# Local attention of a two-layer decoder: in five of its first seven rounds the tensor engine's projections and second arguments stand ahead of the gathers

## The reference, cut to what matters

```python
g = x @ Wg.T + bg                      # 16 heads of 32
v = x @ Wv.T + bv
dot = einsum('bhid,bhjd->bhij', g, g)
corr = dot / (|g_i| * |g_j| + 1e-8) * m        # m: j <= i and j >= i - 128
corr = (corr + 1) / 2
denom = mean_j(corr) + 0.5
fitness = 1 / (denom * sum_i(1 / denom))
attn = softmax(corr * fitness * m + (1 - m) * NEG)
out = (attn @ v) @ Wo.T + bo
```

## Time and profile before

| | |
|---|---|
| Median of 3 runs | 2631.18 us (2628.03 to 2631.48) |
| The profiled execution, whole | 2634.46 us |
| Its span in the trace | 2632.7 us |
| PE busy | 2500.4 us, 95% of the span |
| DVE busy | 2004.3 us, 76% |
| POOL, ACT busy | 864.7 us, 669.0 us |
| Local attention's tiles on PE (arguments) | from 963.4 to 1481.3 us |
| The seven filling rounds | from 963.4 to about 1019.9 us |

### The profile page before, as it was taken

One profiled execution on the slowest core, in us unless ns is written; L12 is line 12 of the kernel. 1 busy time (PEld: TensorE's weight loads), 2 busy tenths in 40 slices (PEclk: granted clock), 3 DMA queues, 4 the chain that ended last, 5 costly groups with the idle time before them and its releaser, 6 DMA issues. The chain is left out here.

```text
span 2632.7 us, 37028 instructions
## 1 busy us (share of the span) xinstructions
PE 2500.4 (95%) x12485; PEld 1550.3 (59%) x12485; DVE 2004.3 (76%) x3404; ACT 669.0 (25%) x961; POOL 864.7 (33%) x900
## 2 busy tenths in 40 slices
PE   8999998999998888999998879999999999999998
PEld 3444544666655434454544447777777777777775
DVE  4899504888877446777778859888888888888886
ACT  1000222222223125666668611000000000000000
POOL 2332103555554336676777611111111111111000
PEclk9999999999999999999999989999999999999999
DMA  6455132222210375555544431222222222222111
GB/s 177 150 167 160 54 108 56 57 59 55 56 41 1 79 152 126 132 130 130 140 111 138 137 101 45 53 54 54 54 55 52 52 52 52 54 54 54 46 39 38
DMA packets 506921, 219.02 MB, mean 83 GB/s; under 512 B 298191, under 2 KB 473679, under 8 KB 505710
## 3 DMA queue, kind: packets, MB, share of 16 engines
q1 hardware_dynamic: 458198, 185.11, 27.6%
q10 hardware_dynamic: 48536, 31.54, 4.7%
HBM read 104.93 MB, written 66.85 MB: 65 GB/s over the span
## 5 line engine op out<-in xcount | busy, mean ns | idle before, releaser
L2216 PE MATMUL bank<-tiles,tl_XQT 128*128 128x512 f32 (+1 forms) x768 | 323.4, 564 | 1.2 <-issue 1.2
L2221 PE MATMUL bank<-tiles,tl_XQT 128*128 128x512 f32 (+1 forms) x768 | 318.0, 557 | 0.0
L2233 PE MATMUL bank<-tiles,tl_HT 128*128 128x512 f32 x682 | 300.8, 596 | 6.0 <-DMA tl_HT<-tl_tmp 6.0
L2216 PEld LDWEIGHTS bank<-tiles,tl_XQT 128*128 128x128 f32 x768 | 235.6, 309 | 79.3 <-issue 15.3
L2221 PEld LDWEIGHTS bank<-tiles,tl_XQT 128*128 128x128 f32 x768 | 236.9, 308 | 65.4
L2233 PEld LDWEIGHTS bank<-tiles,tl_HT 128*128 128x128 f32 x682 | 219.3, 324 | 73.2 <-issue 7.9
L2295 ACT ACTIVATE tl_HQ<-bank 128x512 f32<-128x512 f32 (+1 forms) x96 | 54.0, 562 | 802.1 <-PE bank L2216 756.2
L1493 POOL TENSOR_SCALAR_AFFINE_SELECT tiles<-tiles 128x512 f32<-128x512 f32 x256 | 182.0, 714 | 171.5 <-ACT tiles L1725 154.5
L2163 POOL TENSOR_TENSOR tl_rs<-tl_ve,mhalf 128x1 f32<-128x1 f32 x29 | 16.0, 550 | 526.2 <-DVE tl_ve L2374 526.2
L1498 POOL TENSOR_SCALAR_AFFINE_SELECT tiles<-tiles 128x512 f32<-128x512 f32 x224 | 154.0, 687 | 0.0
L1824 DVE SCALAR_TENSOR_TENSOR tiles<-tiles,bank 128x1024 f32<-128x1024 f32 (+1 forms) x128 | 141.7, 1148 | 15.2 <-PE bank L1600 14.3
(11 more groups left out here) (303 smaller groups left out, 4630.7 us busy)
## 6 DMA issues: line engine op xcount, KB each, us to landing
tl_HT<-tl_tmp SPq DMA_DIRECT2D x248, 44.0 KB, 1.9
tl_HT<-tl_tmp ACTq DMA_DIRECT2D x248, 44.0 KB, 2.0
fp_weights<-space_quant ACTq DMA_DIRECT2D x132, 64.0 KB, 2.0
X<-in_x SPq DMA_DIRECT2D x8, 1024.0 KB, 11.1
v<-tiles SPq DMA_DIRECT2D x32, 256.0 KB, 2.4
unit_g<-tiles SPq DMA_DIRECT2D x32, 256.0 KB, 2.5
unit_gT<-tiles SPq DMA_DIRECT2D x128, 64.0 KB, 2.4
la_GN<-unit_g SPq DMA_DIRECT2D x128, 64.0 KB, 2.1
```

The costliest lines, as they stand in the source:

```text
L2216: mm = e.matmul(bank[(2 * q) % 3][:, 0:w], chunk(XQT[n % 2], c), WgT[q][:, :, c, :], start=(c == 0), stop=(c == C - 1))
L2221: mm = e.matmul(bank[(2 * q + 1) % 3][:, 0:w], chunk(XQT[n % 2], c), WuT[q][:, :, c, :], start=(c == 0), stop=(c == C - 1))
L2233: mm = e.matmul(of_chunks(bank[DOWN][:, :]), chunk(HT, q), WdT[:, q], start=(q == 0), stop=(q == IC - 1))
```

## The change

A round is now a *ramp* round if it prepares tiles, attends to none and isn't late. That holds for rounds 0, 2, 4, 8 and 12. In these, on the tensor engine alone, the projection comes directly behind the first argument, then the second argument, and only then the two gathers. Rounds 6 and 10, and all from round 14 on, keep their order. No instruction is added or removed, and no other engine's list changes.

```diff
                     for n, h in chains:
                         if n is not None:
                             sums(n, h, p)
+
+                    ramp = there(p) and not there(x) and not late
+                    if ramp:
+                        projections(*projected(p), s)
+                        arguments(p + 1)
                     if there(p - 2):
                         gather(p - 2)
                         gather(p - 1)
...
                     if there(x):
                         attend(x)
-                    if there(p):
-                        arguments(p + 1)
-                    projections(*projected(p), s)
+                    if not ramp:
+                        if there(p):
+                            arguments(p + 1)
+                        projections(*projected(p), s)
                     if s in product_at:
                         local_out(product_at[s])
```

## The result

| | before | changed |
|---|---|---|
| Median of 7 runs each | 2631.48 us (2628.03 to 2632.45) | 2640.80 us (2636.34 to 2642.15) |
| Ratio, with its 95% interval | 1 | 1.0031 (1.0022 to 1.0041) |
| Span of the profiled execution | 2632.7 us | 2640.3 us |

The ratio makes +8.2 us (+5.8 to +10.8). I had forecast 2630.7 and a range up to 2635.0. The direction came out as my rival C, to which I had given 7%. The two traces come from long executions: the one of the changed kernel took 2642.15 us, the highest of its seven, and the one of before 2634.46 us, above all seven of before. So traces are compared here by stretches, and whole times by the ratio.

The account below looks back on a forecast made before the run. The tensor engine, busy 95% of 2632.7 us, was taken as the bound. Start-time terms of -7.0, +2.0, +0.8, +4.2 and -0.5 gave -0.5 us, applied to the median 2631.2 for 2630.7 us, range 2627.0 to 2635.0.

Parts of the forecast that it names:

- rival C: Round 12: the clock falls behind two new holes, for scores and dots 2, +5.6 us to 2636.8; chance 7%.
- the one on the clock: Round 2: full clock since the hole ahead shrinks; nothing in the sum, +2.1 us kept for the range.
- rival B: Round 2 or one later hole: the clock is low there, giving 2632.8 to 2634.7 us; chance 23%.
- The fixed point: Round 2: the load of GN1 lets gather 1 start at 976.02, before and after the change.
- Round 0, gain 0: Argument 2 still comes at about 970.5: 1.12 us idle goes, but it must wait for tanh 1.
- Rounds 4 to 10: Lead falls from 7.0 to 5.0 us in round 6 and 4.2 at dots 0; nothing covers z's latency.
- Round 12: Gathers queue behind the g product waiting for scores; gather 11 ends 9.15 us behind the dots, lead 0.
- +4.2 and -0.5: Round 12: the lead of 4.2 us is given back, then dots 2 and 3 end about 0.5 us earlier.
- The sum of the order, -0.5 us: Chain over rounds 0 to 12: terms of -7.0, +2.0, +0.8, +4.2 and -0.5 us; chance 56%.
- the lead of 7.0: Round 2: argument 4 starts at 976.5 against 983.50, 6.0 us of it from the v product.

Follow-up runs that it names:

- The kernel with all holes filled: Changed kernel plus idle products, whose result nobody reads, in all its holes on the tensor engine: ratio to before 1.0009 (1.0000 to 1.0018).
- the kernel with the bias first in all rounds: Changed kernel with unit, bias and turned unit ahead of z on the vector engine in rounds 0, 4, 8 and 12: ratio to before 0.9991.
- the filled kernel before: Kernel before, nothing moved, idle products added ahead of gathers 1 and 9 and between arguments 0 and 1, 10 and 11: ratio to before 1.0000.
- the two filled changed kernels: Changed kernel with idle products in most holes, ratio to before 1.0017, and with more between neighbouring arguments, in all holes, 1.0009.
- The experiment with the bias ahead of z: Changed kernel with unit, bias and turned unit ahead of z on the vector engine in round 12 alone: ratio to before 1.0003 (0.9994 to 1.0013).
- round 2 alone: Kernel before with the new order in round 2 only: ratio to before 1.0007; profiled a second time in one execution, 2629.35 us.

## Why the prediction was wrong, point by point

**The step that failed is the one on the clock**, "I take the better value, since the hole of 4.56 us that stood ahead of the second fall shrinks to about 0.5". That put the clock after the change at nothing in the sum. I weighed the clock at one place, round 2, and took the new holes as rival B, one at a time. Behind the holes of the changed kernel the clock fell five times, each time for 3 to 7 us. The kernel with all holes filled measured what that cost: with the same order and the full clock, 8.6 us less from argument 4 to round 14, and round 14 at +0.1 instead of +9.2 us. Rival C named the mechanism, the two holes of round 12, and priced it at +5.6; it had them at 2.3 and 2.7 us and they are 2.23 and 2.86. I gave it 7% because "rounds 10 and 12 had waits before and kept the full clock". For round 10 of the kernel before these are the rows:

```profile
1005.95 0.64 PE L1574 MATMUL bank<-tiles,la_GN 128*32 128x128 f32 x16 [1.77 <-DMA la_GN<-unit_g]
...
1008.03 0.39 PE L1556 MATMUL bank<-la_RR,la_LR 32*128 32x512 bf16 x2 [1.12 <-ACT tiles L1725]
1008.35 3.70 PE L1662 MATMUL bank<-home_odd,tiles 128*128 128x512 f32 x8
```

That is 2.9 us of idle time within 4 us; in the changed kernel 1.31 for z, 1.65 for the denominators and 1.12 for the second argument, 4.1 us, stand within 7. I had named the larger ones, gave them to rival B as if one alone could cost something, and did not add them up. What makes the clock fall behind one hole and not behind another stays open: it kept up behind the rows above and behind 2.23 us in the kernel with the bias first in all rounds, and it fell behind 0.33 and 0.71 us in the filled kernel before.

**The fixed point** held in number, 976.29, but by luck: the load of GN1 was issued 1.13 us earlier and waited for 1.40 us longer. It was not fixed, as the kernel with the bias first in all rounds shows, where gather 1 starts at 974.43, 1.6 us earlier, with argument 0 only 0.5 us earlier. In the two filled changed kernels it starts at 976.12 and 976.26, the second time straight behind the fillers. But the hole ahead of it was 2.33 us and not 0.5, because the clock did not fall in round 0 of this execution: I had carried the 5.34 us of the g product into round 0 of the changed kernel. It took 3.70, and the v product was ready 1.4 us sooner than I had it.

**Round 0, gain 0**, was wrong by the same: argument 2 came at 969.06, not 970.5. It is of no use, since it only lengthens the hole.

**Rounds 4 to 10** were right at full clock. Argument 4 to dots 0 was foretold as 31.3 us; 31.44 was measured with the clock held up, 35.46 without. In the unfilled changed kernel z waited for the gather, the sums for z (1.30 and 1.31 us), the argument for the denominators.

**Round 12** was right in its waits: g product 4.33 behind the dots (1017.09 - 1012.76 = 4.33), gather 11 behind it, z of chunk 1 behind the gather, the bias behind z, dots 2 waiting for line 1898. At full clock it costs 3.8 us, as the sum had it (+4.2 and -0.5). The experiment with the bias ahead of z showed that its place behind z held up the dots. The Trainium skill ("TensorE: Matmul & The Clock Gate", Architectural detail: the array is 16x 32x32) calls that engine strict FIFO, and 1019.21, 1019.82, 1020.45 in a new order, with the hole gone, agree.

**The sum of the order, -0.5 us**, was set against a kernel before that has falls of its own in round 2. That hid the point. Of the lead of 7.0, 2.2 to 3.0 us were a saved fall: the filled kernel before has argument 4 2.2 us earlier with nothing moved, or 3.0 counted from gather 1. The 4.0 to 4.5 left are the product moved into the wait, and the order gives 3.8 back in the ramp and 3.8 in round 12. So at full clock it costs 3.1 to 3.6.

**What stays open.** How much of a gain in a trace arrives in the whole time. The kernel before with filled holes was 2.8 us ahead of the trace of before in the feed forward and is at 1.0000 in the runs; the changed one with all holes filled was 1.9 us ahead there and measures +2.4. Most of that fits the trace that they are held against: its execution took 2634.46 us, 3.7 above the median of 27 runs of before (2630.73), while the two filled executions took 2631.63 and 2632.50, 0.9 and 1.8 above it. The two executions of round 2 alone show besides that falls move between executions, and 3 us is the size of two falls. I have one trace per kernel but for that one, and no count of falls over many runs, so effects of a few us in the medians aren't explained, only bounded.

## What to carry to other kernels

When work is moved out of a wait, ask what the wait will look like without it: a hole costs more than its length once the clock falls behind it, and here an order that with the clock held up reached round 14 0.1 us late in the trace reached it 9.2 us late without. Add up all holes within one or two rounds, not each alone. And if a producer is moved ahead on one engine, its consumer has to move ahead on the other: the projection was early, its bias still stood behind z, and that exchange of three instructions was worth 6.1 us in round 12 of the changed kernel, more than the 0.5 forecast for the whole change.

## What the runs showed of the hardware

A product of four 128x512 matmuls at 2.4 GHz took 3.70 us in all kernels, to the hundredth; behind some holes it took 4.64 to 6.35. In the changed kernel five stretches of lower clock stood behind idle times of 2.33, 1.41 with 1.12, 1.65 with 1.12, 2.23 and 2.86 us. The same 2.23 us were followed by 3.70 in the kernel with the bias first in all rounds. The Trainium skill ("TensorE: Matmul & The Clock Gate", Part 1: The HAM clock gate) says that throttled is the default and activity releases it; the changed kernel with all holes filled agrees, since products whose result nobody reads were enough to keep 1.00 from 976 to 1030. I had not expected holes this short to do it. Nor that it is partly a matter of the execution: with round 2 alone the same 22 matmuls behind the same wait of 1.85 us took 11.44 us once and 9.74 the other time.
